# Output stage of a fused attention and FFN kernel: two passes change engines, statistics and largest values go by token tile

## The reference

```python
x = x + attention(layernorm(x), ctx)               # ends with  out @ Wo + bo
n = layernorm(x)
scale = sigmoid(clip_x) * max(abs(n)) / 127        # ONE maximum over all 4096 tokens
xq = clip(round(n / scale), -128, 127) * scale
h = silu(xq @ Wg.T) * (xq @ Wu.T)                  # quantised again with one maximum over all of h
x = x + quantised(h) @ Wd.T
```

## Time and profile before

| | us |
|---|---|
| three timed runs, median (lowest to highest) | 1161.38 (1160.01 to 1163.06) |
| profiled execution, its own time | 1157.98 |
| span of its instructions | 1156.2 |
| busy: PE / PEld / DVE / ACT / POOL | 1064.3 / 704.7 / 764.6 / 512.8 / 630.3 |
| output stage, first product to the first operation of the next block | 768.96 to 896.87 |
| mean granted TensorE clock | 0.95 of full |

### The profile page before, as it was taken

How to read it: one execution, slowest core, us unless ns; L and a number is a source line. 1 busy time by engine, 2 the same in 40 slices (tenths; PEclk the granted TensorE clock), 3 DMA queues, 4 the chain that set the end, 5 groups by cost and what they waited for, 6 DMA issues and landing times. The chain is left out here.

```text
span 1156.2 us, 18186 instructions
## 1 busy us (share of the span) xinstructions
PE 1064.3 (92%) x6550; PEld 704.7 (61%) x6550; DVE 764.6 (66%) x1315; ACT 512.8 (44%) x881; POOL 630.3 (55%) x346
## 2 busy tenths in 40 slices
PE   5999999999629989999999999899995799998898
PEld 4888888888516656666666666456663344443343
DVE  5665456654329757777777777138989477877785
ACT  3322223222102657666766677641110555553553
POOL 3433455334440979999999999555434113100373
PEclk9999999999855989999999999899997799999899
DMA  6987677856699897678887774448997353100876
GB/s 205 315 266 238 212 271 255 274 167 198 203 189 189 186 233 159 149 179 177 183 185 170 160 181 115 109 137 220 286 281 190 96 224 122 36 1 2 319 243 218
DMA packets 129619, 218.08 MB, mean 189 GB/s; under 512 B 29320, under 2 KB 55688, under 8 KB 128330
## 3 DMA queue, kind: packets, MB, share of 16 engines
q1 hardware_dynamic: 129546, 217.12, 68.0%
HBM read 134.76 MB, written 77.74 MB: 184 GB/s over the span
## 5 line engine op out<-in xcount | busy, mean ns | idle before, releaser
L783 ACT ACTIVATE a_probs<-a_banks 128x512 f32<-128x512 f32 (+2 forms) x512 | 233.8, 535 | 128.9 <-PE a_banks L991 101.7
L718 POOL TENSOR_TENSOR a_pair_sums<-a_probs,a_probs 128x2048 f32<-128x2048 f32 x48 | 222.1, 4626 | 65.2 <-ACT a_probs L783 57.4
L858 DVE TENSOR_REDUCE a_max<-a_banks 128x2 f32<-128x512 f32 x192 | 123.2, 684 | 52.9 <-PE a_banks L962 52.7
L991 PE MATMUL a_banks<-a_queries,a_keys 97*128 97x512 f32 x384 | 147.8, 428 | 9.1 <-ACT a_probs L783 6.0
L962 PE MATMUL a_banks<-a_keys,a_queries 96*128 96x256 f32 x384 | 86.1, 320 | 32.1 <-DMA a_queries<-q_split 32.1
L967 PE MATMUL a_banks<-a_keys,a_queries 96*128 96x512 f32 (+1 forms) x256 | 115.2, 464 | 0.0
L854 DVE CUSTOM_DVE_ANT_0 a_masked_scores<-a_banks,kept_mask 128x384 f32<-128x384 f32 (+1 forms) x128 | 79.5, 621 | 49.2 <-PE a_banks L967 48.9
L858 DVE TENSOR_REDUCE a_max_parts<-a_banks 128x1 f32<-128x512 f32 x128 | 87.9, 687 | 25.1 <-PE a_banks L967 21.9
L962 PEld LDWEIGHTS a_banks<-a_keys,a_queries 96*128 96x128 f32 x384 | 70.4, 206 | 53.8 <-DMA a_queries<-q_split 32.8
L1347 POOL TENSOR_TENSOR d_out<-d_out,f_x 128x512 f32<-128x512 f32 x28 | 42.6, 1547 | 99.1 <-DVE d_out L1375 99.1
L1231 DVE SCALAR_TENSOR_TENSOR f_h<-g_up,kept_up_scales,f_h 128x512 f32<-128x512 f32 (+1 forms) x88 | 64.2, 746 | 47.2 <-ACT f_h L1196 35.4
(11 more groups left out here) (166 smaller groups left out, 2210.8 us busy)
## 6 DMA issues: line engine op xcount, KB each, us to landing
a_keys<-k_split SPq DMA_DIRECT2D x48, 512.0 KB, 8.2
a_queries<-q_split SPq DMA_DIRECT2D x48, 512.0 KB, 14.2
f_x<-x_scratch SPq DMA_DIRECT2D x14, 1024.0 KB, 7.6
p_c<-in_ctx_dram SPq DMA_DIRECT2D x8, 1024.0 KB, 8.7
p_x<-in_x_dram SPq DMA_DIRECT2D x8, 1024.0 KB, 10.8
v_scratch<-p_v_stage SPq DMA_DIRECT2D x16, 512.0 KB, 8.9
k_split<-p_stage_hi SPq DMA_DIRECT2D x16, 512.0 KB, 4.2
k_split<-p_stage_lo SPq DMA_DIRECT2D x16, 512.0 KB, 5.2
```

Source lines behind the costliest of these rows:

```text
L718: pool.tensor_tensor(PP[u % 2], PR[2 * c % 4], PR[(2 * c + 1) % 4], ALU.add).then_inc(paired, 1)
L783: act.activation(PR[kt % 4][:, j, 0:w], STB[:, n % NST, 0:w], ACT.Exp, scale=SCALE).then_inc(edone, 1)
L858: dve.tensor_reduce(out, src, AX.X, ALU.max).then_inc(wfree, 1)
L991: op = pe.matmul(out.rearrange("p (c t) -> p c t", t=SIT), keys, q, start=True, stop=True)
```

## The change

Two passes over O change engines, and two passes over x1 are cut by token tile:

- `divide(n)` for n of 2 and more goes from VectorE to GpSimd. GpSimd's order becomes `divide(2)`, then for each chunk `norm(n)`, `divide(n + 3)`. Divisions 0 and 1 stay on VectorE.
- `lo(n)` goes from GpSimd to VectorE for all chunks: 0 and 1 ahead of the loop, n + 2 at the end of VectorE's chunk n, behind `kept`.
- VectorE takes the statistics of a tile right after its sum, and waits for that sum first. The fourth sum stands behind the largest values of the chunk before.
- `norm` tells after each tile; the largest value is taken per tile, and `K.amax` has 32 columns in place of 8.
- The semaphore of the first low part goes, and `olo` counts all low parts; SP and TensorE wait for the same low parts as before.

```diff
-            lo_ready(sp, 0)
+            sp.wait_ge(olo, 1)
             load_o(2)
...
-                    lo_ready(sp, n + 1)
+                    sp.wait_ge(olo, n + 2)
                     load_o(n + 3)
...
-            def lo(n):
-                pool.wait_ge(ohi, n + 1)
-                if n >= 2:
-                    pool.wait_ge(full, TT * (n - 1))
-                pool.tensor_tensor(OL[n % 2], OT[n % 2], f32(OH[n % 2]), ALU.subtract).then_inc(olo, 1)
+            def divide(n):
+
+                pool.wait_ge(ldo[n % 2], OLOADS * (n // 2 + 1))
+                pool.tensor_tensor(OT[n % 2], OT[n % 2], RB[n % 2], ALU.mult).then_inc(odiv, 1)
...
                 for t in range(TT):
-                    op = pool.tensor_scalar(XN[u][:, t, :], X1[u][:, t, :], NM[u][:, t:t + 1], RS[u][:, t:t + 1],
-                                            ALU.add, ALU.mult)
-                op.then_inc(xn, 1)
+                    pool.tensor_scalar(XN[u][:, t, :], X1[u][:, t, :], NM[u][:, t:t + 1], RS[u][:, t:t + 1],
+                                       ALU.add, ALU.mult).then_inc(xn, 1)
...
-            lo(1)
+            divide(2)
             for n in range(NCH):
-                if n + 2 < NCH:
-                    lo(n + 2)
                 norm(n)
+                if n + 3 < NCH:
+                    divide(n + 3)
...
+            def lo(n):
+                dve.wait_ge(ohi, n + 1)
+                if n >= 2:
+                    dve.wait_ge(full, TT * (n - 1))
+                dve.tensor_tensor(OL[n % 2], OT[n % 2], f32(OH[n % 2]), ALU.subtract).then_inc(olo, 1)
+
             def chunk(n):
...
-                    dve.wait_ge(xn, n - 1)
+                    dve.wait_ge(xn, TT * (n - 1))
                 for t in range(TT):
+                    if n and t == TT - 1:
+                        chunk_largest(n - 1)
                     dve.wait_ge(full, TT * n + t + 1)
                     dve.tensor_tensor(X1[u][:, t, :], BK[:, TT * u + t, :], X[u][:, t, :], ALU.add).then_inc(free, 1)
-                if n + 2 < NCH:
-                    divide(n + 2)
-                dve.wait_ge(free, TT * (n + 1))
-                for t in range(TT):
+                    dve.wait_ge(free, TT * n + t + 1)
                     op = dve.bn_stats(ST[:, t, :], X1[u][:, t, :])
                 op.then_inc(chain, 1)
...
                 dve.tensor_copy(K.rs2[:, TT * n:TT * (n + 1)], RS[u][:, :]).then_inc(kept, 1)
+                if n + 2 < NCH:
+                    lo(n + 2)
 
             def chunk_largest(n):
-                dve.wait_ge(xn, n + 1)
-                dve.tensor_reduce(K.amax[:, n:n + 1], XN[n % 2], AX.XY, ALU.max, apply_absolute_value=True).then_inc(amd, 1)
+                for t in range(TT):
+                    dve.wait_ge(xn, TT * n + t + 1)
+                    op = dve.tensor_reduce(K.amax[:, TT * n + t:TT * n + t + 1], XN[n % 2][:, t, :], AX.X, ALU.max,
+                                           apply_absolute_value=True)
+                op.then_inc(amd, 1)
...
-            dve.wait_ge(ohi, 1)
-            dve.tensor_tensor(OL[0], OT[0], f32(OH[0]), ALU.subtract).then_inc(olo_first, 1)
+            for n in range(2):
+                lo(n)
             for n in range(NCH):
                 chunk(n)
-                if n:
-                    chunk_largest(n - 1)
                 if n == 1:
                     invert(BATCH - 1)
```

More of the change, by code:

```diff
@@ L559, in attend_output @@
         dloaded, drec, rstored = s.sem("dens_loaded"), s.sem("dens_inverted"), s.sem("reciprocals_stored")
-        odiv, ohi, olo_first, olo = s.sem("o_divided"), s.sem("o_hi"), s.sem("o_lo_first"), s.sem("o_lo")
+        odiv, ohi, olo = s.sem("o_divided"), s.sem("o_hi"), s.sem("o_lo")
         full, free = s.sem("bank_full"), s.sem("bank_free")
@@ L582, in slot_pieces @@
             return list(range(first, first + S_PER_SLOT[kt]))
-        def lo_ready(eng, n):
-            if n:
-                eng.wait_ge(olo, n)
-            else:
-                eng.wait_ge(olo_first, 1)
         @blk.sync
@@ L1086, in _ @@
             for m in range(NCH):
-                lo_ready(pe, m)
+                pe.wait_ge(olo, m + 1)
                 chunk(m, n)
@@ L1461, in xattn_ffn @@
         K.ones, K.row = s.sb("ones", [P, DH]), s.sb("ones_row", [1, P])
-        K.nm2, K.rs2, K.amax = s.sb("neg_mean2", [P, T // P]), s.sb("rstd2", [P, T // P]), s.sb("x1_largest", [P, NCH])
+        K.nm2, K.rs2, K.amax = s.sb("neg_mean2", [P, T // P]), s.sb("rstd2", [P, T // P]), s.sb("x1_largest", [P, T // P])
         K.fs, K.fsc = s.sb("ffn_row_scale", [P, NCH, FJ + 1]), s.sem("ffn_scales_stored")
```

## The result

| | before | after |
|---|---|---|
| median of nine timed runs each, us | 1158.98 (1157.48 to 1163.06) | 1154.82 (1152.12 to 1157.16) |
| ratio, 95% interval | | 0.995 (0.9937 to 0.9964) |
| profiled execution: own time / span, us | 1157.98 / 1156.2 | 1155.27 / 1153.5 |
| first product of the stage, from the start of the span | 768.96 | 770.66 |
| from there to the first product of chunk 7 | 102.06 | 98.09 |

Faster by 4.2 us in the medians, 0.4%; the ratio of the runs is 0.995, with an interval that lies under 1. The stage itself gained 4.66 us; the span gained 2.7, since in this execution the attention part ahead of the stage ended 1.7 us later and the part behind it took 0.3 us more.

What follows compares the result with a forecast made beforehand. VectorE, at 15.0 us a chunk against TensorE's 13.4, made O's low part late. 3.5 (chunk 7) + 1.3 (the end) - 0.1 = 4.7 us, off the timed 1161.38: 1156.7, range 1151.5 to 1164.0 us.

Steps and rivals of the forecast that it cites:

- The exchange: Divisions 2 to 7 leave VectorE (2.29 us each) for GpSimd (4.6); low parts 1 to 7 come to VectorE (2.29).
- Rival D: GpSimd multiplies at 6 us or more, 1.4 more on each path: 1159.5 us, chance 0.05.
- The stall: VectorE's means instruction L906 stops waiting (3.78 us) for GpSimd, except in chunk 0, whose statistics are copied 1.6 us earlier.
- The collision: Low part on VectorE meets GpSimd's normalisation: it waits one tile, 0.65 us, and the normalisation waits 2.2 us for it.
- Rival A: Four normalisation tiles pass as one, each low part waits 3.0 us: 3.2 us slower, 1164.6 us, chance 0.12.
- Interleaving: VectorE's sums and statistics alternate: 1.32 us a tile, 5.3 a chunk; cost 0.3 us a chunk, gain in last only.
- Largest values in pieces: VectorE's largest value per tile: 4 x 0.6 = 2.4 us instead of 2.29; wait for normalisation covered by 1.5 us.
- Loads and the path behind them: O loads land 19.8 us behind the store, then 8.1 us to copied statistics; chunk 3's come 5.7 us earlier.
- Rival B: Reciprocals land 3 to 4 us later than forecast, so chunk 7 starts at 871.2: 1159.8 us, chance 0.14.
- Chunk 7: Chunk 7 starts 34.2 us after chunk 3's statistics are copied, at 867.5, keeping 3.5 of the 5.7 us.
- The end: Behind the last sum one statistics and one largest piece remain; next stage 892.1 instead of 896.87, adding 1.3 us.
- rival C: Low parts precede normalisations or loads land 2 us earlier; lower clock's 1.5 us also goes: 1153.2 us, chance 0.17.

Runs made afterwards that it cites:

- order only: Kernel before, with GpSimd normalising chunk n first and making the low part of n + 2 behind it, no pass changing engine: 1160.4 us, ratio 1.0019.

## Why the prediction was right, point by point

The forecast was 1156.7 us and 4.7 less than before; measured were 1154.82 and 4.2 less. The gap in the absolute time is the anchor: the three runs that I had gave 1161.38 for before, nine give 1158.98.

1. *The exchange.* Division 4.6 us as taken, no bound needed; high part 1.92. Rival D (a slow multiplication) is out.
2. *The stall.* Gone as said, with the one in chunk 0 left (2.99). The tile cut alone shows that it would only have moved.
3. *The collision.* This term was mis-sized: the low part waited 0 us, not 0.65, and so took 2.29. The other half was right: the first tile took 2.88 to 2.91 and the normalisation 5.14 (5.2 forecast). Rival A needed a wait of 2 us and had 0. Two subtractions lay over the 6.93 us of the earlier trace rows, of which the prediction names the second; the first, of the same line and size, ran from 21.52 to 23.80.
4. *Interleaving.* 1.32 us a tile, as worked out.
5. *Largest values in pieces.* 2.45 us; no wait at the fourth sum.
6. *Loads and the path behind them.* From landing to kept 8.0 us (825.04 to 832.99), forecast 8.1. The landings came 17.9 and 18.3 us behind the store, not 19.8 and 20.6, so kept(3) stood at stage time 62.3, 2.0 us earlier than the 64.3 that I took. Rival B is out: nothing landed later than forecast.
7. *Chunk 7.* kept(3) to chunk 7 took 35.8 us, forecast 34.2: the x load 0.5 more, the transpose 12.86 instead of 11.0, the low part 0.65 less. kept(3) was 2.0 us ahead of the forecast, but the transpose started only 1.5 ahead and took 1.9 more, so it ended 0.3 behind the forecast: all of that gain was given back. Chunk 7: 4.0 earlier, forecast 3.5. What I took from before unchanged, 14.9 us for the chunk, was 16.3: the stretch at the lower clock lasted 6.8 us, before 3.4, behind waits of 4.32 and 3.56. The exchange alone had 3.4 behind a wait of 4.75, so the length of the wait alone doesn't set it; what does stays open.
8. *The end.* Put on the start of the stage before (minus 1.70), last sum 883.7, kept(7) 887.35, last largest value 890.9, store landed 891.7, next block 892.2. The forecast had 883.7, 887.2, 890.9, 891.6 and 892.1. This held although the last product ended 0.9 us later than forecast, because VectorE was still behind it, but narrowly: its last sum started 0.4 us behind the bank (885.03, 885.42), where the forecast had 1.3.

So the total came out close in part by luck, since each error met one of the other sign: 2.0 and 0.65 us better on the way to chunk 7, 2.4 worse in the transpose's path. What the forecast names as the mechanism, the stall gone and the load queue next, is what the runs show. The first half of rival C (loads earlier, low parts unhindered) was there too, with kept(3) at its 831.3 when counted from the start of the stage before; its gain went into the transpose, and the clock went the other way. Steps 6 and 7 named the wait of root behind the division, but only in a term of 2.2 us; taking it out moved chunk 7 by 3.7, most of it through chunk 0, which step 2 had inside kept(0) = 792.0 (measured 792.0) without a price of its own. A slip in rival B changes nothing: chunk 7 at 871.2 is 0.2 us later than before, so its sum is 1160.0 and not 1159.8.

## What to carry to other kernels

When a small operation stalls beside another engine's long one, moving the small one in time can just hand the stall to its neighbour (the tile cut alone: L906 at 0.17 us, L464 at 4.28). Moving the long one cleared the stall (order only: 0.17 in all chunks), but its result then came late for TensorE. The exchange works since it gives GpSimd a pass that can lie behind its normalisation and still be in time; both exchanged passes read two tensors in SBUF as before. So look for the place of the long instruction where neither the small ones nor the next product need that time, and check with a run that the stall is gone and not moved. A longer operation put ahead of a short one that others wait for (division, high part, root) is paid on every engine that waits for the short one, so look at once for the order that lets the short one pass. And follow the chain on to the queue that fills the buffers: here more than the whole change brought (5.5 us) lay in two lines that only say behind which chunk a long transpose is issued.

## What the hardware showed that I had not expected

- A small instruction is shut out as long as a large one: 128x4 operations of 0.16 us took 3.8 (one input, TENSOR_SCALAR) and 4.28 to 4.35 us (two inputs) beside a GpSimd instruction of 4.5 us. Sums from PSUM, batch-norm statistics and reductions took their usual 0.68, 0.69 and 2.45 beside the same GpSimd instructions.
- A recorded start on GpSimd doesn't tell who has the port: 0.11 us after it VectorE still got in first (2.29 us, GpSimd's tile 2.88), 0.42 us after it VectorE took 0.20 longer (2.49) and the tile its usual 0.77.
- The issue of each of the two transposes of the stage held SP's queue for 10.2 to 17.0 us in these kernels, 12.86 and 16.03 in after, and that of a load of the scales between 0.4 and 8.7 us. What is queued behind waits for the issue and not for the landing: in after the loads of O go out at 847.38, as the issue ends, and the transpose lands at 849.4.
